# Graph attention logits as four narrower products on four column groups, and the last layer's row factors moved from SBUF to two PSUM banks

## The reference

```python
m = jax.nn.leaky_relu(x_j + x_r[tgt] + e_emb, NEG_SLOPE)   # (edges, 4 heads, 32)
logits = jnp.einsum('ehc,hc->eh', m, att)
# then a softmax per target node, a weighted sum, gelu, two layer norms
```

```python
agg = jax.ops.segment_sum(x[src], dst, num_segments=N_NODES)
h = jax.nn.relu(agg @ W.T) + h_in
return _layernorm(x + h)
```

## Time and profile before

| | us |
|---|---|
| median of 3 runs | 3164.38 (3162.36 to 3165.82) |
| the profiled execution | 3169.91 |
| its span (first to last instruction) | 3168.1 |

### The profile page before, as it was taken

How to read it: one execution, slowest core, us unless ns; L and a number is a source line. 1 busy time by engine, 2 the same in 40 slices (tenths; PEclk the granted TensorE clock), 3 DMA queues, 4 the chain that set the end, 5 groups by cost and what they waited for, 6 DMA issues and landing times. The chain is left out here.

```text
span 3168.1 us, 46332 instructions
## 1 busy us (share of the span) xinstructions
PE 2503.6 (79%) x14131; PEld 1745.7 (55%) x14131; DVE 2587.8 (82%) x3230; ACT 2089.9 (66%) x3726; POOL 1869.3 (59%) x1771
## 2 busy tenths in 40 slices
PE   7899999959999968888888699999999753345500
PEld 3466666637677756666665466777777542234400
DVE  6689999969999959999999457898888747999900
ACT  0176767746666648888888589999999744545500
POOL 4477777723344427777775556555555007777776
PEclk9999999979999989999999899999999855666855
DMA  7456767657677756777776448888988538984211
GB/s 210 114 176 222 222 217 229 214 167 219 207 215 220 216 161 209 231 233 233 232 232 206 118 138 212 217 210 206 236 213 213 153 101 275 277 275 136 81 40 39
DMA packets 495087, 611.79 MB, mean 193 GB/s; under 512 B 66865, under 2 KB 284651, under 8 KB 494716
## 3 DMA queue, kind: packets, MB, share of 16 engines
q1 hardware_dynamic: 433030, 495.63, 52.0%
q0 software_dynamic: 56480, 111.88, 13.6%
q10 hardware_dynamic: 5334, 1.32, 0.2%
HBM read 391.94 MB, written 220.55 MB: 193 GB/s over the span
## 5 line engine op out<-in xcount | busy, mean ns | idle before, releaser
L1848 POOL DMA_INDIRECT f_rows<-table_x,src_row x196 | 228.9, 1168 | 225.2 <-POOLq L1249 165.8
L1328 POOL DMA_INDIRECT g_xd_xs<-table_x,dst_row x196 | 199.0, 1015 | 263.9 <-PE g_psT L1396 170.1
L781 POOL DMA_INDIRECT c_xs<-table_x,src_row x196 | 187.3, 956 | 261.9 <-PE c_psT L923 209.4
L771 POOL DMA_INDIRECT c_xs<-table_h,src_row x196 | 221.3, 1129 | 121.4 <-issue 78.9
L503 POOL DMA_INDIRECT xs<-in_x,src_i x196 | 227.1, 1159 | 86.6 <-issue 55.5
L488 POOL DMA_INDIRECT xd<-in_x,dst_i x196 | 216.9, 1106 | 94.8 <-issue 47.6
L1328 POOL DMA_INDIRECT g_xd_xs<-table_x,src_row x196 | 205.0, 1046 | 59.7 <-issue 59.7
L1855 POOL DMA_INDIRECT out<-f_rows,end_i x196 | 197.1, 1006 | 62.4 <-issue 62.1
L1900 PE MATMUL f_psT<-w_ident,f_rows 128*128 128x128 f32 x196 | 48.5, 393 | 219.9 <-DVE f_rows L1993 219.9
L771 POOL DMA_INDIRECT c_xd<-table_h,dst_row x196 | 185.1, 944 | 59.7 <-issue 59.7
L1401 PEld LDWEIGHTS g_psP<-w_center,g_turns 128*128 128x128 f32 x1568 | 183.8, 191 | 49.6 <-ACT g_turns L1537 28.3
(11 more groups left out here) (338 smaller groups left out, 8457.2 us busy)
## 6 DMA issues: line engine op xcount, KB each, us to landing
g_share<-shares SPq DMA_DIRECT2D x196, 192.0 KB
xn<-in_x SPq DMA_DIRECT2D x49, 512.0 KB
table_x<-xo SPq DMA_DIRECT2D x49, 512.0 KB, 2.9
table_x1b<-xb SPq DMA_DIRECT2D x49, 512.0 KB, 4.9
c_xn<-table_x SPq DMA_DIRECT2D x49, 512.0 KB
table_h<-c_xo SPq DMA_DIRECT2D x49, 512.0 KB
c_xn<-table_h SPq DMA_DIRECT2D x49, 512.0 KB
c_x1r<-table_x1b SPq DMA_DIRECT2D x49, 512.0 KB
```

Of the source, the lines that this page charges most:

```text
L771: pool.indirect_dma_start(out=quarters(rows[:, s, :])[j], out_offset=None, in_=table, in_offset=edge_index(columns, now.n, j)).then_inc(la ...
L781: pool.indirect_dma_start(out=quarters(xs[:, s, :])[j], out_offset=None, in_=table, in_offset=edge_index(h.src_row, now.n, j)).then_inc(sr ...
L1328: pool.indirect_dma_start(out=quarters(xd_xs[:, s, k, :])[j], out_offset=None, in_=table, in_offset=edge_index(columns, now.n, j)).then_in ...
L1848: pool.indirect_dma_start(out=quarters(rows[:, n, :])[j], out_offset=None, in_=table, in_offset=edge_index(h.src_row, n, j)).then_inc(src_ ...
```

## The change

In the third layer each of the two 512-column products is cut into two of 256 columns. The four products have `att_a` (32 columns) as their weights and write to the four groups of 32 partitions of `psA`, all in columns 0 to 255. The copy `alike` is now 128 x 256 in place of 36 x 512 elements, each half is stored by its own transfer (four transfers of 4 x 256 in place of two of 4 x 512), and the semaphore counts double. In the last layer `rstdn` and `rstde` are columns of two PSUM banks, until now unused, in place of SBUF tensors; `rstd`, the last factor, stays in SBUF.

```diff
-        alike = sb("alike", [36, 2, TILE])
+        alike = sb("alike", [P, 2, TILE // 2])
...
                     for i in range(2):
-                        sp.dma_start(logits[s, i, :, k * TILE:(k + 1) * TILE],
-                                     alike[32 * i:32 * i + heads, (c - 1) % 2, :]).then_inc(alike_stored[(c - 1) % 2], 16)
+                        for half in range(2):
+                            at, part = k * TILE + half * TILE // 2, 32 * (2 * i + half)
+                            sp.dma_start(logits[s, i, :, at:at + TILE // 2], alike[part:part + heads, (c - 1) % 2, :]
+                                         ).then_inc(alike_stored[(c - 1) % 2], 16)
...
-                        sp.wait_ge(alike_stored[i], 32 * ((c - 1 - i) // 2 + 1 if c - 1 >= i else 0))
+                        sp.wait_ge(alike_stored[i], 64 * ((c - 1 - i) // 2 + 1 if c - 1 >= i else 0))
...
-                    nc.tensor.matmul(psA[0:32, 0, :], att_a[:, :], zl[:, :], start=True, stop=True).then_inc(a_ready, 1)
-                    nc.tensor.matmul(psA[32:36, 0, :], att_a[:, 0:heads], zsl[:, :], start=True, stop=True).then_inc(a_ready, 1)
+                    for i, leaky in enumerate((zl, zsl)):
+                        for half in range(2):
+                            part, cols = 32 * (2 * i + half), slice(half * TILE // 2, (half + 1) * TILE // 2)
+                            nc.tensor.matmul(psA[part:part + 32, 0, 0:TILE // 2], att_a[:, :], leaky[:, cols],
+                                             start=True, stop=True).then_inc(a_ready, 1)
...
-                    act.wait_ge(a_ready, 2 * c)
-                    wait(act, alike_stored[(c - 1) % 2], 32 * ((c - 1) // 2))
-                    nc.scalar.activation(alike[:, (c - 1) % 2, :], psA[0:36, 0, :], ACT.Copy).then_inc(a_kept, 1)
+                    act.wait_ge(a_ready, 4 * c)
+                    wait(act, alike_stored[(c - 1) % 2], 64 * ((c - 1) // 2))
+                    nc.scalar.activation(alike[:, (c - 1) % 2, :], psA[:, 0, 0:TILE // 2], ACT.Copy).then_inc(a_kept, 1)
...
-                    wait(dve, a_ready, 2 * c)
+                    wait(dve, a_ready, 4 * c)
...
-        varn, lnvn, rstdn = (sb(n, [P, 16]) for n in ("varn", "lnvn", "rstdn"))
-        sqe, vare, lnve, rstde = sb("sqe", [P, 2, TILE]), sb("vare", [P, 8]), sb("lnve", [P, 8]), sb("rstde", [P, 8])
+        varn, lnvn = (sb(n, [P, 16]) for n in ("varn", "lnvn"))
+        sqe, vare, lnve = sb("sqe", [P, 2, TILE]), sb("vare", [P, 8]), sb("lnve", [P, 8])
...
+        node_factors, edge_factors = bank("node_factors"), bank("edge_factors")
+        rstdn, rstde = node_factors[:, 0:16], edge_factors[:, 0:8]
```

## The result

| | us, median (range, runs) | profiled execution | its span | mean granted clock |
|---|---|---|---|---|
| before, same chip | 3165.10 (3162.36 to 3167.53, 4) | 3169.9 | 3168.1 | 0.904 |
| changed | 3143.94 (3138.40 to 3149.68, 4) | 3149.68 | 3147.9 | 0.902 |

The ratio is 0.9932, 95% interval 0.9914 to 0.9950. A second set of five runs gave 3143.06 us and 0.9929 (0.9915 to 0.9943). The forecast was 3137.3 us with a range of 3131 to 3150: right in sign, a quarter too large in size (27.1 us forecast; 0.68% of 3164.4 is 21.5).

A forecast was written before the change was run, and what follows sets the result against it. GpSimd was taken to bound the last 550 us, a loop across engines the third layer. Gains of 20.5 and 6.6 us gave 3142.8 from the profiled 3169.9, 3137.3 from the median 3164.4; range 3131 to 3150 with the first rival.

The forecast's parts named there:

- What holds GpSimd: Last layer: VectorE instructions with two SBUF inputs stall GpSimd's gathers and scatters; slow gathers lose 44 us.
- GpSimd stays held: Last layer: any long VectorE multiplication stalls gathers, wherever its second input lies; only the third layer gains, 3158 us, chance 0.07.
- Gathers end at 2865: Last layer: gathers from 2611 take 245 us, plus 9 us for 17 steps still held by the `rstd` multiplication.
- The last node pair's store is next: Last layer: the first scatter then waits for that store's landing, at 2881 instead of 2899.7, gaining 18.7 us.
- The factors in PSUM cost nothing: Last layer: VectorE reads and ScalarE writes factors in PSUM at unchanged speed; bounds 12 us either way over 25 steps.
- the rival at 3217: Last layer: broadcasting a factor from PSUM runs at half speed, the last pair is stored 80 us later; chance 0.03.
- The scatters, 1.8 us shorter: Last layer: first to last scatter shortens by 1.8 us, with 5.3 us still lost to holds by the `rstd` multiplication.
- The third layer, 0.20 us in 33 steps: Third layer: the shorter copy `alike` lets the affine copy start 0.20 us sooner in 33 steps, 6.6 us.
- the further gain to 13 us: Third layer: upper bound, 0.40 us in each of 33 steps, if the shorter products help once more.
- The rival of four groups one after the other: Third layer: the four products run in sequence, 0.8 us more a step; 3170 us in all, chance 0.03.
- SyncE's two more transfers: Third layer: 0.6 us more behind `g_alike` each step, covered by the node-row load's wait; cost 0, if uncovered 4 us.
- The sum against the time: Whole kernel: 20.5 us from the last layer and 6.6 from the third, giving 3137.3 us from 3164.4.

The follow-up runs named there:

- the shifted edge tiles: Changed kernel with the last layer's edge tiles handled four steps later than the node pairs: 3125.49 us; also run with the third factor in PSUM, four or six steps.
- the logits alone: Kernel before with only the third layer's split products, smaller copy and transfers, the factors left in SBUF: 3159.40 us, ratio 0.9977.
- the narrow copy: Changed kernel with the copy to `alike` cut from 256 to 32 columns, so most logits are left out: 3139.62 us, ratio 0.9914 to the kernel before.
- the third set: Changed kernel with the third layer's four logits products issued three times, only the last set signalling: 3159.48 us, against 3140.33 when issued twice.

## Why the prediction was right, and where it was off

- *What holds GpSimd: right.* Two inputs in SBUF, not the length: L2008 lasts 2.28 us and holds nothing, L2018 lasts 0.68 and does; moving its factor too frees the rest. Of the two statements in the Trainium skill's page "SBUF — State Buffer", section "Who interferes with whom", these rows agree with the one on two SBUF inputs against a GpSimd instruction that reads SBUF. The inference beside it, that a `tensor_tensor` leaves the writing of descriptors alone, doesn't cover these indirect gathers: one took 2.50 us beside it. The rival "GpSimd stays held" fell with this.
- *Gathers end at 2865: 2861.8.* 16 of them were held, for 7.3 us in all; 17 and 9 us were forecast.
- *The last node pair's store is next: right.* Released by its landing, the first scatter started 269.4 us after the first gather; forecast 270, gain 19.3 against 18.7.
- *The factors in PSUM cost nothing: right.* 2.280 us against 2.284 for the broadcast from PSUM that no row had shown, 0.69 and 0.68 for the two shorter ones. With it the rival at 3217 fell. They even gained a little: ScalarE writes the edge factors to PSUM in 0.180 us in place of 0.209, and the pair steps take 10.44 us in place of 10.48.
- *The scatters, 1.8 us shorter: nothing.* 258.3 us before and after (257.6 to 258.3 in the other traces with both factors in PSUM and `rstd` in SBUF, without the shifted edge tiles). GpSimd, held once a tile, still keeps VectorE's pace; only the instruction that holds it changed from L1995 to L2018, and the first steps had no faster stretch. Freeing both gives 4.5.
- *The third layer, 0.20 us in 33 steps: right in size, by two errors that cancel, and wrong in one place of its account.* Most steps that gained did so by 0.15 to 0.18 us, but there were 36 of them: the whole layer shows 6.2 of 6.6 us, the logits alone 5.3 in the trace and 7 us by the times. I read the start of the turn as the end of the products; it was the end of the copy to `g_nodeT`, which also came 0.1 us ahead of it (2233.11 + 1.01 = 2234.12 in that trace, the turn at 2234.22). So the shorter products gave nothing, and the further gain to 13 us was not to be had: the turn took back 0.04 of the copy's 0.21 us, and of the next 0.18 us, with the narrow copy, all. The rival of four groups one after the other didn't come true, and its price was about right: the third set made the turn 0.41 us late and the layer 16.9 us longer (727.6 against 710.7). At that rate, an estimate, 0.8 us would cost 33 us against the changed kernel and 27 against the one before; the prediction had 26.
- *SyncE's two more transfers: no cost.* The logits alone came out as forecast without one, and its loads' wait for L1778 fell to 61.2 us (79.1 before).
- *The sum against the time.* Over the two layers the profile gives 25.5 us of the 27.1; the medians give 21.5 and 22.5. In the two profiled executions the difference is the 5.3 us lost in stretches that the change doesn't touch. For the medians, where 3 to 4 us are missing, it isn't shown where they went; the first stretch alone ends between 1779.9 and 1792.5 in the traces.

## What to carry to other kernels

When an engine's queue is free to run but its instructions are now and then long, line up the long ones with what a neighbour engine does at that moment, and look at where the neighbour's inputs lie; a factor of a few columns moved into a spare PSUM bank can be worth more than the arithmetic around it. Before counting such a gain, find what the released queue will wait for next: here half of it went into the wait for the last node pair, and only reordering the other work (edge tiles later) turned it into time. A reordering that shortens one kind of step has to be priced in the other kind as well: 0.4 us in each of 18 steps ate what four steps had gained. And an instruction that starts when another ends need not wait for it: look in the code for the semaphore, or double the suspect and see whether the time moves.

## What the runs showed of the hardware

- Four fp32 products of 256 columns on four groups of 32 output columns run at the same time on TensorE: all four make a pass every 0.215 us, two passes a product, 0.43 us a set back to back, at a granted clock of 1.00, the level of 2.4 GHz.
- VectorE reads a factor broadcast over 128 columns from PSUM as fast as from SBUF: 2280 against 2284 ns for 2048 elements a partition. ScalarE writes 8 factors a partition to PSUM in 180 ns, to SBUF in 208 to 209.
- In the two rows read, a held gather ends 0.82 us after VectorE's instruction does, whatever was left of that when it started: 2.50 us beside the 2.28 of L2001, 1.40 beside the 0.68 of L2018 (2703.98 against 2703.16), 0.94 without.
- The DMA engines reached 345 GB/s over 40 us at a share of 0.99 when loads and stores of 512 KB ran beside indirect gathers.
